# A two-layer attention kernel: which engine adds the softmax sums, values in quarters, and four images in a loop body

## The reference, cut to what matters

```python
f = xf @ wf + bf                       # 4096 x 8
g = xf @ wg + bg                       # 4096 x 8
hh = xf @ wh + bh                      # 4096 x 64
s = jnp.einsum('bnk,bmk->bnm', g, f)   # 4096 x 4096 scores an image
attn = jax.nn.softmax(s, axis=-1)
o = jnp.einsum('bnm,bmc->bnc', attn, hh)
return gamma * o.reshape(b, h, w, c) + x
```

## Time and profile before

| what | value |
|---|---|
| median of 3 runs | 3980.12 us (3980.10 to 3980.86) |
| profiled execution | 3977.29 us |
| its span, first to last instruction | 3975.3 us |
| granted TensorE clock, mean of the span | 0.981 of 2.4 GHz |
| PE, PEld busy | 97%, 37% |
| DVE, ACT, POOL busy | 80%, 70%, 49% |
| chain that ended last | PE 72%, issue 16%, POOL 6%, DVE 3%, ACT 3% |

### The profile page before, as it was taken

The page is one execution under the profiler, slowest core; times in us unless marked ns, Lnnn a source line. Parts: engine busy times, 40 slices in busy tenths (PEclk is TensorE's granted clock), DMA queues, the critical chain, the costliest instruction groups (busy, mean ns, idle before and its releaser), DMA issues.

```text
span 3975.3 us, 81252 instructions
## 1 busy us (share of the span) xinstructions
PE 3869.3 (97%) x26001; PEld 1476.7 (37%) x26001; DVE 3185.5 (80%) x6206; ACT 2790.6 (70%) x3642; POOL 1943.7 (49%) x1031
## 2 busy tenths in 40 slices
PE   5999999999999999999999999999999999999999
PEld 3223442244422443224432254323443235422444
DVE  5778887788877888778877798777987779877888
ACT  1567776677766777767776777767776677767777
POOL 3696108941099311991139910498006961079510
PEclk7899999999999999999999999999999999999999
DMA  1000000000000000000000000000000000000000
GB/s 35 1 1 23 1 1 12 1 23 1 12 1 1 22 1 11 1 1 22 1 12 1 5 19 1 12 1 18 6 1 12 1 23 1 1 12 1 22 1 12
DMA packets 13910, 33.47 MB, mean 8 GB/s; under 512 B 3941, under 2 KB 3941, under 8 KB 12133
## 3 DMA queue, kind: packets, MB, share of 16 engines
q1 hardware_dynamic: 13540, 28.57, 2.5%
HBM read 11.78 MB, written 8.39 MB: 5 GB/s over the span
## 4 chain that ended last, share of the span: by engine, by line
PE 72%; issue 16%; POOL 6%; DVE 3%; ACT 3%; SPq 0%; POOLq 0%; DVEq 0%; DMA 0%; ACTq 0%
PE sum_banks L619 22%; PE score_banks L607 21%; PE sum_banks L515 13%; PE score_banks L499 7%; POOL e_sum L396 6%; PE sum_banks L537 2%; PE sum_banks L471 2%; ACT e_whole L808 1%; PE score_banks L463 1%; ACT g_tr L785 1%; DVE tile_max L979 1%; DVE e_whole L1147 1%; PE sum_banks L556 1%; PE score_banks L482 0%; PE score_banks L447 0%
## 5 line engine op out<-in xcount | busy, mean ns | idle before, releaser
L979 DVE TENSOR_REDUCE tile_max<-sum_banks 128x1 f32<-128x512 f32 (+1 forms) x2128 | 1367.9, 686 | 506.1 <-PE sum_banks L471 501.0
L396 POOL TENSOR_TENSOR e_sum<-e_sum,e_whole 128x1024 f32<-128x1024 f32 x704 | 1660.3, 2358 | 97.0 <-ACT e_whole L808 51.1
L808 ACT ACTIVATE e_whole<-score_banks,no_bias,down 128x1024 f32<-128x1024 f32 x1024 | 1228.9, 1204 | 516.8 <-PE score_banks L499 461.5
L875 ACT ACTIVATE e_whole<-e_whole,exp_bias 128x1024 f32<-128x1024 f32 x1024 | 1175.9, 1148 | 447.9 <-DVE e_whole L1147 430.4
L1147 DVE TENSOR_SCALAR_CACHE_REDUCE e_whole<-score_banks,neg_down 128x1024 f32<-128x1024 f32 x1024 | 1293.0, 1282 | 94.5 <-PE score_banks L607 83.9
L515 PE MATMUL sum_banks<-e_whole,proj 128*64 128x512 f32 x4096 | 1118.1, 625 | 0.0
L619 PE MATMUL sum_banks<-e_whole,v_scaled 128*64 128x512 f32 x4096 | 1054.6, 593 | 0.0
L607 PE MATMUL score_banks<-k_high,q_split 128*64 128x512 f16 x4096 | 806.9, 380 | 2.3 <-DVE e_whole L1147 1.9
L607 PE MATMUL score_banks<-k_low,q_split 128*64 128x512 f16 x4096 | 805.2, 379 | 0.0
L471 PE MATMUL sum_banks<-f_tr,g_tr 33*128 33x512 f16 x2128 | 688.1, 399 | 15.1 <-DVE tile_max L979 9.7
L499 PE MATMUL score_banks<-g_tr,f_tr 34*128 34x512 f16 x2048 | 634.9, 389 | 18.3 <-issue 9.0
(11 more groups left out here) (132 smaller groups left out, 1650.6 us busy)
## 6 DMA issues: line engine op xcount, KB each, us to landing
x_in<-in_x_dram SPq DMA_DIRECT2D x11, 1024.0 KB, 5.0
out_dram<-y_out SPq DMA_DIRECT2D x32, 256.0 KB, 2.7
k_high<-k_high SPq DMA_DIRECT2D x32, 128.0 KB, 2.2
k_low<-k_low SPq DMA_DIRECT2D x32, 128.0 KB, 2.2
w<-in_L_conv_wg_dram SPq DMA_DIRECT2D x2, 2.0 KB
w<-in_L_conv_wf_dram SPq DMA_DIRECT2D x2, 2.0 KB
w<-in_L_conv_wh_dram SPq DMA_DIRECT2D x2, 16.0 KB
b<-in_L_conv_bh_dram SPq DMA_DIRECT2D x1, 32.0 KB
```

Source lines behind the costliest of these rows:

```text
L396: nc.gpsimd.tensor_tensor(acc, acc, e_whole[:, i % U0, :], ALU.add).then_inc(e_added, 1)
L808: nc.scalar.activation(e_whole[:, i % U0, :].rearrange("p (a n) -> p a n", a=2), score_banks[:, 2 * (i % 2):2 * (i % 2) + 2, :], ACT.Exp, ...
L875: nc.scalar.activation(e_whole[:, u, :], e_whole[:, u, :], ACT.Exp, bias=exp_bias[:, u:u + 1], scale=-1.0, accum_out=part_sum[:, u // NCH, ...
L979: nc.vector.reduce_max(tile_max[:, blk, j:j + 1], sum_banks[:, (2 + j % banks) % 4, :], AX_X).then_inc(a_used, 1)
```

## The change: what it does

- **Ninth tile to PE.** POOL no longer adds tile 30 (`NINTH`): 22 additions a chunk, and PE sums nine tiles.
- **Pairs.** Tiles 3 and 7, 11 and 15, 19 and 23 are added by DVE, tile by tile, into a new buffer `e_pair` (`pair_probs`, 128x1024 f32, both inputs in SBUF), behind the max tiles of steps 9, 17 and 25. PE sums `e_pair` behind the values of tiles 9, 17 and 25 (steps 13, 21, 29) in place of the six tiles. Tiles 27, 30 and 31 are summed singly. ACT waits for the pair before it overwrites one of its tiles, and DVE for PE's sum of the last pair (`pair_summed`).
- **Values in quarters.** `values0` becomes four matmuls with 32 columns of weights, in the same four strips of rows as the sums.
- **`split_max`** stands in POOL's order ahead of tile 22's addition (23 isn't POOL's).
- **Four images in a loop body** (`UNROLL`), on PE, ACT, DVE and POOL.

```diff
+    UNROLL = 4
...
+    NINTH = T - 2
+    PAIR, PAIRS0 = 2 * GROUP, 3
+    PAIR_AT, PAIR_SUM = 2, 2
+    ADDS = T // GROUP * (GROUP - 1) - 2
...
         def on_pool(i):
-            return i % GROUP != GROUP - 1
+            return i % GROUP != GROUP - 1 and i != NINTH
+
+        def pair_of(i):
+
+            return i // PAIR if i < PAIRS0 * PAIR and not on_pool(i) else None
...
                         for i in range(T):
-                            if i == LAST:
-                                split_max((two * 2 + par) * NCH + q + 1, par * NCH + q + 1)
+                            if i == LAST - 2:
+                                split_max(image * NCH + q + 1, par * NCH + q + 1)
...
-                for half in range(2):
-                    mm = nc.tensor.matmul(sum_banks[half * C:(half + 1) * C, 0, :], proj[:, par, i, GFW:PW],
+                for c in range(SUMS):
+                    rows = slice(c * (P // SUMS), (c + 1) * (P // SUMS))
+                    half, part = c // 2, c % 2
+                    mm = nc.tensor.matmul(sum_banks[rows, 0, :],
+                                          proj[:, par, i, GFW + part * (C // 2):GFW + (part + 1) * (C // 2)],
                                           e_whole[:, i % U0, half * BANK:(half + 1) * BANK], start=i == 0, stop=i == T - 1,
                                           skip_group_check=True)
                 if i == T - 1:
                     mm.then_inc(v0_full, 1)
                     return
-                if on_pool(i):
+                if on_pool(i) or pair_of(i) is not None:
                     mm.then_inc(pv0_done, 1)
-                    return
-                if i == GROUP - 1:
-                    pe.wait_ge(mid_ready, image * NCH + q + FREE)
-                sum_of(e_whole[:, i % U0, :], i == GROUP - 1, False).then_inc(pv0_done, 1)
+                else:
+                    sum_of(e_whole[:, i % U0, :], False, False).then_inc(pv0_done, 1)
+                if i >= PAIR and i % PAIR == PAIR_SUM - 1 and i // PAIR <= PAIRS0:
+                    if i == PAIR + PAIR_SUM - 1:
+                        pe.wait_ge(mid_ready, image * NCH + q + FREE)
+                    pe.wait_ge(e_paired, (image * NCH + q) * PAIRS0 + i // PAIR)
+                    sum_of(e_pair[:, :], i // PAIR == 1, False).then_inc(pair_summed, 1)
...
-                    if on_pool(i) and i >= U0:
+                    if i >= U0 and pair_of(i - U0) is not None:
+                        act.wait_ge(e_paired, (image * NCH + q) * PAIRS0 + pair_of(i - U0) + 1)
+                    if i >= U0 and on_pool(i - U0):
                         act.wait_ge(e_added, (image * NCH + q) * ADDS + adds_with(i - U0))
...
+            def pair_probs(image, q, n):
+                first, second = n * PAIR + GROUP - 1, n * PAIR + 2 * GROUP - 1
+                dve.wait_ge(exp0_done, image * NCH * T + q * T + second + 1 + FREE_ST)
+                dve.wait_ge(pair_summed, (image * NCH + q) * PAIRS0 + n + FREE)
+                nc.vector.tensor_tensor(e_pair[:, :], e_whole[:, first % U0, :], e_whole[:, second % U0, :], ALU.add
+                                        ).then_inc(e_paired, 1)
...
+                    if i >= PAIR and i % PAIR == PAIR_AT - 1 and i // PAIR <= PAIRS0:
+                        pair_probs(image, q, i // PAIR - 1)
```

More of the change, by code:

```diff
@@ L79, in attention_pair_kernel @@
     PIECES_AT = BPC // 2
-    assert BPC == EARLY * (T // U0) and B % 2 == 0
+    assert BPC == EARLY * (T // U0) and B % UNROLL == 0
     assert U0 == U1 and N % (P * BPC) == 0 and C == 64 and CK == 8 and NCH == 4
@@ L127, in attention_pair_kernel @@
         ones_w = sb("ones_w", [P, P // SUMS], F32)
-        credit = sb("credit", [P, 14], F32)
+        credit = sb("credit", [P, 15], F32)
         proj = sb("proj", [P, 2, T, PW], F32)
@@ L148, in attention_pair_kernel @@
         e_sum = sb("e_sum", [P, 2, CH], F32)
+        e_pair = sb("e_pair", [P, CH], F32)
         d_sb = sb("d_sb", [P, SQ], F32)
@@ L200, in attention_pair_kernel @@
         e_added = sem("e_added")
+        e_paired, pair_summed = sem("e_paired"), sem("pair_summed")
         v_scaled_ready = sem("v_scaled_ready")
@@ L210, in on_pool @@
         def on_pool(i):
-            return i % GROUP != GROUP - 1
+            return i % GROUP != GROUP - 1 and i != NINTH
+        def pair_of(i):
+            return i // PAIR if i < PAIRS0 * PAIR and not on_pool(i) else None
         def adds_with(i):
-            return max((GROUP - 1) * (i // GROUP) + i % GROUP, 1)
+            return max(sum(on_pool(k) for k in range(i + 1)) - 1, 1)
         pair_a, pair_b = score_banks[:, 0:2, :], score_banks[:, 2:4, :]
@@ L305, in _ @@
             for n, (free, by) in enumerate(((y_act, FREE_Y), (y_dve, FREE), (mid_ready, FREE), (y_stored, 16 * FREE),
-                                               (v0_copied, FREE))):
+                                               (v0_copied, FREE), (pair_summed, FREE))):
                 nc.gpsimd.memset(credit[:, 8 + n:9 + n], 0.0).then_inc(free, by)
@@ L402, in _ @@
             split_max(0, 0)
-            with pool.Fori(0, B // 2) as two:
-                for par in range(2):
+            with pool.Fori(0, B // UNROLL) as some:
+                for k in range(UNROLL):
+                    image, par = some * UNROLL + k, k % 2
                     for q in range(NCH):
                         for i in range(T):
-                            if i == LAST:
-                                split_max((two * 2 + par) * NCH + q + 1, par * NCH + q + 1)
+                            if i == LAST - 2:
+                                split_max(image * NCH + q + 1, par * NCH + q + 1)
                             if on_pool(i):
-                                add_probs(two * 2 + par, q, i)
-                    second_layer(two * 2 + par, par)
+                                add_probs(image, q, i)
+                    second_layer(image, par)
         @block.tensor
@@ L775, in image_steps @@
                 turn_back(image)
-            with pe.Fori(0, B // 2) as two:
-                for par in range(2):
-                    image_steps(two * 2 + par, par)
+            with pe.Fori(0, B // UNROLL) as some:
+                for k in range(UNROLL):
+                    image_steps(some * UNROLL + k, k % 2)
         @block.scalar
@@ L803, in chunk0 @@
                     act.wait_ge(pv0_done, step + 1)
-                    if on_pool(i) and i >= U0:
+                    if i >= U0 and pair_of(i - U0) is not None:
+                        act.wait_ge(e_paired, (image * NCH + q) * PAIRS0 + pair_of(i - U0) + 1)
+                    if i >= U0 and on_pool(i - U0):
                         act.wait_ge(e_added, (image * NCH + q) * ADDS + adds_with(i - U0))
-                    elif on_pool(i) and q > 0:
+                    elif i < U0 and q > 0 and on_pool(T + i - U0):
                         act.wait_ge(e_added, (image * NCH + q - 1) * ADDS + adds_with(T + i - U0))
@@ L897, in image_steps @@
                                    ).then_inc(y_act, 1)
-            with act.Fori(0, B // 2) as two:
-                for par in range(2):
-                    image_steps(two * 2 + par, par)
+            with act.Fori(0, B // UNROLL) as some:
+                for k in range(UNROLL):
+                    image_steps(some * UNROLL + k, k % 2)
         @block.vector
@@ L1201, in image_steps @@
                                           sum_banks[:, j, :]).then_inc(y_dve, 1)
-            with dve.Fori(0, B // 2) as two:
-                for par in range(2):
-                    image_steps(two * 2 + par, par)
+            with dve.Fori(0, B // UNROLL) as some:
+                for k in range(UNROLL):
+                    image_steps(some * UNROLL + k, k % 2)
 _INS = ['x', 'L0_conv_wf', 'L0_conv_bf', 'L0_conv_wg', 'L0_conv_bg', 'L0_conv_wh', 'L0_conv_bh', 'L0_conv_gamma',
```

1 line of the change is left out of this document (removed).

## The result

The changed kernel takes 4087.4 us (median of four runs, 4083.2 to 4096.5), the kernel before 3980.5 in the same session: a ratio of 1.0274, with a 95% interval of 1.0261 to 1.0287. It is slower, as forecast, but by 2.7% where 0.6% was forecast, and the time lies 2.4 us above the range. The profiled execution took 4089.4 us, with a span of 4087.4.

A forecast was written before the change was run, and what follows sets the result against it. PE (busy 56.7 of 57.66 us a chunk) and POOL (54.7) are both nearly full, PE ahead. The profiled 3977.3, +32 for eight images, -5.9 for loop gaps make 4003.4, predicted as 4003 us; range 3938 to 4085.

The forecast's parts named there:

- The split: Step 26: `max_rows` waits less for POOL, gain 0.8 us a chunk with q > 0, 1.3 with q = 0.
- the sums: PE's sums behind values, now in the same strips: 0.45 us each instead of 0.57, gain 1.74 a chunk with q > 0.
- the quarters: PE's values as four streams: 1.00 us a tile instead of 1.01, bounds 0.98 and 1.05, gain 0.3 a chunk.
- step 8: Two tiles' values follow each other on PE without the sum between: the second costs 0.86 us, not 1.01, gain 0.15.
- the meeting of DVE and POOL: At SBUF the two take turns; the pairs' additions take about 1.4, 3.1 and 1.3 us, 1.22 where none waits.
- The four images: Where the loop starts again: two of three 2.94 us gaps of PE go, -5.9 us.
- The third pair: DVE's addition behind step 25: asks near the end of POOL's turn at tile 22's addition and waits 0.1 us.
- the stop in step 19: PE waits there for DVE's max tiles behind the second pair's addition and loses 2.7 us.
- a rival at 0.25: The clock falls as well: PE's stop in step 19 costs 3.3 us a fall; 4030 to 4110, taken 4065; chance 0.25.
- The second pair: DVE's addition behind step 17: waits 1.9 us for tile 16's, margin 0.3; rival: slips ahead, W 0, 3942 us, chance 0.20.
- The third pair late by a phase: Rival: 0.4 us later it meets tile 24's addition, W 2.2 instead of 0.1, +67, 4070 us; chance 0.08.

The follow-up runs named there:

- run 1: The changed kernel without the pairs, PE summing all nine tiles one by one: 3917.6 us, ratio 0.9844.
- run 2: The changed kernel with DVE's pair addition replaced by a maximum over one 128x1024 tile, same places and waits: 3927.5 us, ratio 0.9871.
- run 3: The changed kernel with POOL's additions cut to 8 of 1024 columns, their number, order and waits kept: 3929.6 us, ratio 0.9879.
- run 6: The changed kernel with the pairs' additions one step later, behind the max tiles of steps 10, 18 and 26: 4115.9 us, ratio 1.0359.
- run 5: The changed kernel without the pairs, DVE reducing a constant 128x1024 buffer three times behind step 17's max tiles: 4064.6 us, ratio 1.0215.
- run 7: The changed kernel with the third pair alone, added behind step 25, PE summing the other tiles one by one: 3984.4 us, ratio 1.0010.

## Why the prediction came out as it did

**What held.** The split, the sums and the quarters came out to 0.1 us: a sum behind values in the same strips costs 0.43 (steps of 1.97 to 1.99 against 1.53 to 1.56; 0.45 taken), two tiles' values in a row in step 8 save 0.15 (3.00 us with the sum between them in run 1, 2.42 here, less the sum's 0.43), a plain step went from 1.547 to 1.534. So did the meeting of DVE and POOL, which no row of before showed for this operation: 1.47, 3.17 and 1.56 us against 1.4, 3.1 and 1.3. Runs 2 and 3 show that it is POOL's turn that DVE waits for. The four images gave 5.2 of 5.9 us; one gap is left, behind the fourth image (timeline of PE, the first scores of the second loop body):

```profile
2104.86 0.38 PE L510 MATMUL score_banks<-g_tr,f_tr 34*128 34x512 f16 x1 [2.87 <-issue]
```

**What was a little off.** Where the clock stays, a chunk takes 58.92 us; 58.6 was forecast. Steps 9 and 25 take 1.67 us and not 1.53: their second max tile now waits for DVE, since the sum that used to give DVE half a microsecond of rest there is gone (run 1 shows step 9 at 1.53 and step 25 at 1.56; in run 6, with the pairs behind other steps, they still take 1.67 and 1.66). I had charged DVE for what the change adds and not for the slack that it takes away. And step 6 takes 2.56 us instead of 2.42, in run 1 as well, for which I had no term. The third pair waited 0.35 us instead of 0.1.

**The step that failed** is that the sum leading to 4003 put the clock at nothing. It had the stop in step 19 right (2.7 us forecast, 2.75 measured), took the clock to be kept through it, and left the fall to a rival at 0.25; the range even leaves out a fall in most chunks. The runs showed a fall in 21 of 24 chunks with q > 0 and more of them in chunks q = 0, some 79 us in all. Against the forecast of 4003.4, the profiled execution's 4089.4 are 86 us more. The 24 chunks with q > 0 sum to 1445.3 us; at their own lengths with the clock kept (16 x 58.92 + 8 x 56.86 = 1397.6) the clock makes up 47.7. The missed 0.3 us makes 8. Chunks q = 0 took 503.5 us together, 464.9 before, of which 8 were forecast: 31 more, and there the clock falls a second and third time: it is at half for 139 us of these chunks, 79 before, and half of the difference is 30. Two of these chunks in the changed kernel (before: 0.91 to 0.94):

```profile
2600.54:2666.84 66.30, 61.42 (x397) 12.36 (x399) 47.60 (x69) 39.27 (x33) 53.47 (x25) 0.82 0.05 17
3098.42:3160.53 62.11, 56.80 (x397) 12.22 (x399) 47.71 (x69) 39.27 (x33) 53.51 (x25) 0.89 0.06 18
```

The three terms sum to 87. Without the clock's two the time would be about 4010, inside the range and 0.2% from the forecast: the rest of the mechanism was right, and "slower" held for its reasons.

I gave the rival 0.25, and wrote against it that the stop is shorter than the stretch in the earlier trace rows, and that a wait of 1.3 us had kept the clock. Neither decides: step 19 holds PE for 2.75 us more than a plain step, between the 1.3 that kept the clock and the 4.4 that lost it, and I let the kinder row speak. Run 5 shows that a stop of 3.0 us is enough, runs 6 and 7 that 1.8 can be. The rival's price was 3.3 us a fall, in six chunks of ten. In chunks with q > 0 a fall cost less, 1.5 us (60.4), 3.1 (62.05) or once 4.4 (63.34), but 21 of 24 had one; in chunks q = 0 it came to 3.9 us each. With those numbers (21 x 2.3 us, and 31 for chunks q = 0) the rival comes to about 4082 instead of 4065, and it is the case that came; the measured time lies inside its bounds of 4030 to 4110.

**The other rivals.** The second pair did meet tile 16's addition in every chunk; with q > 0 DVE asked 0.27 to 0.30 us behind its start, the margin of 0.3 that was forecast, and with q = 0 up to 1.1. That it can slip past is shown by run 6 (1.21 us), and that it pays only as long as the clock stays. The third pair late by a phase is shown by run 7.

## What to carry to other kernels

Work put on an engine that others wait for is priced by three things: its own length less the slack at that place, the turn that it must wait for at a shared port, and what the stop does to TensorE's clock; here these were 1.7, 2.5 and 2.0 us a chunk with q > 0, for 1.4 us of saved sums. When a new stop of PE lies between one that kept the clock in the trace and one that lost it, the fall is no outside case, and every stop of that size in the program has to be counted. And two engines that are both nearly full have to be relieved together: the parts one by one gave 18 of the 62 us.

## What the runs showed of the hardware that I had not expected

- The same program keeps the clock in one chunk and loses it in the next, in one execution: 59.24 us at 1.00 and 61.79 at 0.94 in run 5, 58.92 and 62.05 in the changed kernel. Page "TensorE: Matmul & The Clock Gate" of the Trainium skill (Part 1) says that the block that gates the clock watches TensorE on its own schedule, which doesn't start with the kernel; these runs agree in so far as the same program in the same execution gives both, and none of them shows the schedule itself.
- A fall of the clock can feed itself, since POOL and DVE keep their pace while PE is at half: in run 6 it moved the next pair from 1.21 to 3.23 us. But a fall isn't needed for that: asking 0.01 to 0.02 us behind POOL's start, DVE went ahead in 13 chunks and waited 2.2 us in four.
- POOL waits its turn as well. In the changed kernel its additions have a mean of 2.487 us, 2.358 before: one that starts behind DVE's ends 0.8 us late.
- A maximum over 1024 elements from SBUF takes 1.208 us and an addition of two such tiles 1.214 where nothing holds it (run 3); beside POOL's additions of 2.36 us the first stays at 1.208, and the second takes up to 3.43 (run 6).
